# Dequantising weights by accumulating DMAs: negated zeros loaded first, the integer weights added on top

## The reference

```python
def dequantize(imatrix, scales, zeros, group_size, out_dtype):
    rs = jnp.repeat(scales, group_size, axis=0)
    rz = jnp.repeat(zeros, group_size, axis=0)
    return ((imatrix.astype(rs.dtype) - rz.astype(rs.dtype)) * rs).astype(out_dtype)
...
gate = jax.nn.silu(jnp.dot(x, gate_proj))
up = jnp.dot(x, up_proj)
return jnp.dot(gate * up, down_proj)
```

## Time and profile before

| | |
|---|---|
| three timed executions | 434.56, 435.77, 436.81 us, median 435.77 |
| profiled execution | 434.57 us |
| its span, first to last instruction | 432.8 us (1.8 us lie around it) |
| PE busy | 410.4 us, 95% of the span |
| DVE, ACT, POOL busy | 330.4, 330.5, 265.8 us |
| granted TensorE clock | 0.996 of full speed |

### The profile page before, as it was taken

One profiled execution on the slowest core, in us unless ns is written; L12 is line 12 of the kernel. 1 busy time (PEld: TensorE's weight loads), 2 busy tenths in 40 slices (PEclk: granted clock), 3 DMA queues, 4 the chain that ended last, 5 costly groups with the idle time before them and its releaser, 6 DMA issues.

```text
span 432.8 us, 10751 instructions
## 1 busy us (share of the span) xinstructions
PE 410.4 (95%) x4228; PEld 317.9 (73%) x4228; DVE 330.4 (76%) x582; ACT 330.5 (76%) x540; POOL 265.8 (61%) x264
## 2 busy tenths in 40 slices
PE   7878988999988999999999999999999999999994
PEld 5655666777856777777777878677877888888872
DVE  4778666998878778788887777787887667667676
ACT  2438898897877788687778888687888998988970
POOL 3335797899588654665473954755566555555561
PEclk9899999999999999999999999999999999999999
DMA  7677746966742000002010000000000000001003
GB/s 255 190 230 259 279 147 226 300 204 209 241 121 69 2 11 16 26 2 76 12 39 26 2 0 27 27 2 26 26 27 0 2 1 9 17 24 50 1 1 97
DMA packets 26792, 35.44 MB, mean 82 GB/s; under 512 B 1870, under 2 KB 18422, under 8 KB 26742
## 3 DMA queue, kind: packets, MB, share of 16 engines
q1 hardware_dynamic: 26434, 34.71, 24.5%
q10 hardware_dynamic: 244, 0.05, 0.1%
q0 software_dynamic: 64, 0.00, 0.0%
HBM read 30.56 MB, written 4.19 MB: 80 GB/s over the span
## 4 chain that ended last, share of the span: by engine, by line
PE 73%; DVE 9%; issue 6%; POOL 6%; ACT 4%; DMA 1%; POOLq 0%; SPq 0%; DVEq 0%; ACTq 0%
PE banks L764 20%; PE banks L766 19%; PE banks L777 10%; PE banks L778 9%; PE banks L663 4%; DVE yT L1039 2%; PE banks L703 2%; ACT banks L555 2%; PE banks L692 2%; PE banks L673 2%; PE banks L681 2%; POOL t_sb L416 1%; DVE st L925 1%; PE banks L722 1%; DVE qkT L943 1%
## 5 line engine op out<-in xcount | busy, mean ns | idle before, releaser
L555 ACT ACTIVATE banks<-banks,ratio 128x512 f32<-128x512 f32 x336 | 207.8, 664 | 34.9 <-PE banks L766 25.4
L1039 DVE SCALAR_TENSOR_TENSOR yT<-banks,sd,yT 128x512 f32<-128x512 f32 x208 | 154.1, 746 | 48.8 <-PE banks L778 48.1
L764 PE MATMUL banks<-xT,wgu 128*128 128x512 f32 x448 | 182.2, 407 | 5.2 <-DVE t_sb L1024 2.5
L766 PE MATMUL banks<-xT,wgu 128*128 128x512 f32 x448 | 175.1, 391 | 0.0
L416 POOL TENSOR_TENSOR t_sb<-t_sb,u_sb 128x512 f32<-128x512 f32 x56 | 72.7, 1298 | 63.1 <-DVE t_sb L1024 63.0
L764 PEld LDWEIGHTS banks<-xT,wgu 128*128 128x128 f32 x448 | 84.1, 188 | 27.6 <-issue 3.7
L766 PEld LDWEIGHTS banks<-xT,wgu 128*128 128x128 f32 x448 | 84.3, 188 | 15.2
L777 PE MATMUL banks<-hr,wd 128*128 128x512 f32 x224 | 89.3, 399 | 4.2 <-DVE yT L1039 2.3
L778 PE MATMUL banks<-hr,wd 128*128 128x512 f32 x224 | 87.5, 390 | 0.0
L429 POOL TENSOR_TENSOR hr<-t_sb,hr 128x512 fp32r<-128x512 f32 x56 | 73.1, 1305 | 5.1 <-ACT hr L577 0.7
L777 PEld LDWEIGHTS banks<-hr,wd 128*128 128x128 f32 x224 | 42.0, 188 | 19.3 <-DVE yT L1039 9.5
(11 more groups left out here) (93 smaller groups left out, 383.9 us busy)
## 6 DMA issues: line engine op xcount, KB each, us to landing
x_sb<-in_x SPq DMA_DIRECT2D x16, 256.0 KB, 5.2
out<-x_sb SPq DMA_DIRECT2D x16, 256.0 KB, 2.1
wgu_in<-in_L_ffn_gate_w SPq DMA_DIRECT2D x7, 512.0 KB, 5.7
z_in<-in_L_ffn_gate_z SPq DMA_DIRECT2D x7, 512.0 KB, 5.4
wgu_in<-in_L_ffn_up_w SPq DMA_DIRECT2D x7, 512.0 KB, 5.5
z_in<-in_L_ffn_up_z SPq DMA_DIRECT2D x7, 512.0 KB, 5.0
wd_in<-in_L_ffn_down_w SPq DMA_DIRECT2D x7, 512.0 KB, 5.3
z_in<-in_L_ffn_down_z SPq DMA_DIRECT2D x7, 512.0 KB, 4.6
```

The costliest lines, as they stand in the source:

```text
L555: act.activation(banks[:, bank, :], banks[:, bank, :], ACT.Copy, scale=ratio[:, m, g, it:it + 1]).then_inc(done[n % 2], 1)
L764: pe.matmul(banks[:, bank, :], w, xT[:, c % 2, 0, g, :], start=g == 0, stop=False, skip_group_check=True)
L766: pe.matmul(banks[:, bank, :], w, xT[:, c % 2, 1, g, :], start=False, stop=True, skip_group_check=True).then_inc(full[n % 2], 1)
L1039: dve.scalar_tensor_tensor(y, bank, sd[:, it, b:b + 1], y, ALU.mult, ALU.add).then_inc(s_free, 1)
```

## The change

The pass on the compute engines is gone. ACT's queue loads the three small tables of zeros (int32), ACT changes their sign and makes them f32, and SP writes them to a table `z_out` in HBM. From there SP loads each piece's zeros, broadcast to 128 partitions, straight into the place of the weights. Then POOL issues a DMA that reads the integer weights from HBM and adds them there (`accum_op=ALU.add`). PE waits for that DMA's semaphore. `z_in`, the two DVE waits on weights in `take_down` and all waits of SP for zero buffers are gone; the places in `piece_after` differ.

```diff
-    piece_after = {q: EARLY + i for i, q in enumerate((0, 2, 4, 9, 11, 14, 19, 21, 25, 27, 32, 33, 37, 38, 43, 44, 47))}
+    piece_after = {q: EARLY + i for i, q in enumerate((0, 2, 4, 8, 9, 12, 15, 16, 19, 21, 24, 26, 28, 31, 33, 36, 38))}
...
+            sync.wait_ge(s_zneg, 1)
+            sync.dma_start(z_out[:, :].rearrange("m (p n) -> p m n", n=64), z_neg).then_inc(s_zout, 16)
+            sync.wait_ge(s_zout, 16)
+
+            load_zeros(0)
+            load_zeros(1)
+            for k in range(2, EARLY + 1):
+                (load_ctx if k % 2 else load_x)(PRE + (k - 2) // 2)
+                sync.wait_ge(s_w[k - 2], 16)
                 load_zeros(k)
...
-                pool.tensor_tensor(piece_of(wgu_in, wd_in, k), piece_of(wgu_in, wd_in, k), piece_z(k),
-                                   ALU.subtract).then_inc(s_dif, 1)
+                pool.wait_ge(s_z[k], 16)
+                pool.dma_start(piece_of(wgu, wd, k), w.rearrange("(g p) n -> p g n", p=P),
+                               accum_op=ALU.add).then_inc(s_w[k], 16)
...
             norm1(0)
+            act.wait_ge(s_zraw, 48)
+            act.activation(z_neg, z_raw.bitcast(I32), ACT.Copy, scale=-1.0).then_inc(s_zneg, 1)
             norm1(1)
...
-            def convert(k):
-                act.wait_ge(s_dif, ready(k)[1])
-                act.copy(piece_of(wgu, wd, k), piece_of(wgu_in, wd_in, k)).then_inc(s_deqa, 1)
...
-                dve.tensor_tensor(piece_of(wgu, wd, k)[:, g, :], piece_of(wgu_in, wd_in, k)[:, g, :],
-                                  piece_z(k)[:, g, :], ALU.subtract).then_inc(s_deqv, 1)
```

## The result

The changed kernel takes 432.75 us (median of 7, 430.33 to 433.91) against 435.77 us before: ratio 0.9922, 95% interval 0.9894 to 0.9951. It is faster by 0.8%; the medians differ by 3.0 us. The profiled execution took 432.93 us, with a span of 431.1 us against 432.8, so this one shows 1.7 us of it.

The account below looks back on a forecast made before the run. PE was taken as the bound, idle in chunk 0 through dequantising; -1.3 (start) - 5.0 (chunk 0) + 1.0 (POOL) + 0.5 (prologue) = -4.8 us, giving 431.0 us as median, range 426.5 to 445.

Parts of the forecast that it names:

- near 97: Sign of being right: chunk 0, from `product` 0 to 14, takes near 97 us, against 101.33 before.
- the landing times grew: Sign of being wrong: landing times of the weight pieces that grow; no size given.
- Chunk 0, -5.0: Chunk 0: with dequantising gone from DVE and ACT, its whole loss against chunk 1's pace is recovered, -5.0 us.
- DMA time, "0": Weight pieces: accumulating DMAs of 3.1 us each stay hidden behind the matmuls, up to 4.2 us bearable; cost 0.
- PE would wait for `s_w`: Late places, if accumulating DMAs are too slow: at 4.6 us a piece 7 us late, about 438; chance 0.10.
- The start, -1.3: Step 0: without ACT's conversion the first `rescale` starts at about 46.2 instead of 47.54, -1.3 us.
- POOL's issue, 1.0: POOL's weight DMAs: each issue takes 1.0 us, 14 of them from place 6 to 38, leaving POOL 89% full.
- POOL's limit: Place 6 to 38: POOL becomes the bound at 1.4 us per issue.
- a fuller POOL (+1.0): Between `gated` and the down matmuls: POOL's fuller queue adds +1.0 us.
- Rival (1): Place 6 to 38: POOL becomes the bound; at 2.4 us per issue +7.6 us, 443; chance 0.17.
- The prologue, +0.5: Before place 0: `weigh(0)`, ending by 18.2, stays hidden; +0.5 us added for a new chain of five DMA landings.
- Rival (2): Place 6 to 38: DVE holds up POOL's issues, 1.9 us each; 436.4 us, no change; chance 0.06.

Follow-up runs that it names:

- no_zeros: Changed kernel with weight DMAs as plain converting copies, no zeros loaded and no POOL wait for them (result lacks the zeros): 425.4 us, ratio 0.9789.
- late_x: Changed kernel with the loads of x tiles 9 to 15 moved behind the last zeros in SP's program: 427.9 us, ratio 0.983.
- old_places: Changed kernel with the table of places of the kernel before: 434.0 us, ratio 0.9985.
- copy_only: Changed kernel with the weight DMAs as plain converting copies, without the addition; zeros loaded but not counted: 428.2 us, ratio 0.986.
- quiet_start: late_x with SP held before the zeros of piece 7 until PE has done `values(4)`: 427.9 us, ratio 0.984.
- late_x_split: late_x with each piece's accumulating DMA issued as two halves, 21 more issues for the same bytes: 434.7 us, ratio 0.9992.
- late_x_old_places: late_x with the table of places of the kernel before: 436.6 us, ratio 1.0026.

## Why the prediction was right, and where it was not

The direction and the interval held: 432.75 us in 426.5 to 445, faster. The forecast of 431.0 was 1.8 us too low; of the 4.8 us in the sum 3.0 came. The interval is wide: it reaches 9 us above the kernel before. And the parts agree less well than the sum. In the profile chunk 0 gave 0.7 us of 5.0 (100.6 us, where "near 97" was named as the sign of being right), the landing times grew, which was named as a sign of being wrong, and 0.6 us came from the prologue, where +0.5 was forecast. That the direction held with a stall of some 5 us in chunk 0 is in part luck.

**Chunk 0, -5.0.** The size was right as a ceiling, a little low: 6.3 us in no_zeros, 6.0 in late_x. The reading that led to it, chunk 0 against chunk 1 at the same points of the pattern, holds. In the changed kernel only 0.7 us of it arrived, and with the table of places of the kernel before (old_places) no gain in time is left: the new places are a part of what was gained.

**DMA time, "0".** This is the step that failed: it cost some 5 us (chunk 0 took 100.6 us, and 95.3 in late_x). The size of a piece was good: 3.1 us forecast for an accumulating one, 3.2 measured. The reduce rule of the Trainium skill (Collectives: The Full Stack, "The bandwidth ceiling"), half the rate of a copy, which was measured there on rings of four ranks, agrees with that against the 1.5 us of SP's copies; against a converting copy issued by POOL itself the addition costs 3.2 to 2.0, a factor of 1.6 here. What was wrong is the stretch over which I spread it. I divided by the 107 us from the first issue to the last use. But POOL issues its 17 pieces between 43.6 and 121 us: 17 x 3.2 = 54 us, zeros of 16 pieces at (0.173 x 431.1 - 0.089 x 425.8)/21 = 1.75 us (the SP queue with and without zeros) 28 us, 14 tiles some 11 us: 93 us of work for 77 us (an estimate; the shares of the two queues in that stretch, 0.657 and 0.464, give 87). So the engines were full and a queue grew. I also looked for the lateness only at PE's wait for the weights, where the lead is 11 places or more. The item with the short lead is the zeros: they share a queue with x tiles that nobody needs yet, and the wait for them stands on POOL, ahead of `rs` and `product`. "PE would wait for `s_w`" named the wrong waiter: PE waited for DVE's `yT`, DVE for POOL's `rs`, POOL for the zeros. PE does wait for the weights once the issues are late, as the two runs with the old table show.

**The start, -1.3.** The first `rescale` came as forecast, at 45.62, 0.1 us after its matmul (before, 1.4 us after). From place 0 to `product` 0, counted from PE's first matmul, only 11.2 - 10.9 = 0.3 us remained of it: PE's run of `score` had the gap of 1.01 us, whose cause is open. In copy_only, no_zeros and quiet_start, without the gap, that stretch took 9.6 us, 1.6 less than before: there the term is whole.

**POOL's issue, 1.0.** It took 1.31 us for gate and up and 1.2 for down, close below the 1.4 where I put POOL's limit. POOL was busy 50.5 us between `product` 0 and 8, forecast 50.9, and that agreement is luck: 13 pieces are issued in that stretch and not 14 (piece 20 stands behind `product` 8), each took 0.2 to 0.3 us more than forecast, and many overlapped the next instruction (the `product` of 75.19 starts 0.5 us before the issue of 74.36 is over). The cost of a fuller POOL (+1.0) can't be read off alone; late_x still got 6.0 of 6.3 us, so it is at most 0.3 where nothing stalls. Rival (1) did not come, but late_x_split shows that it was one doubling away. (At 2.0 us per issue its sum is 36.9 + 28.0 = 64.9, not 65.1.)

**The prologue, +0.5.** `weigh(0)` ran from 17.71 to 19.29, later than my 17.2 to 18.2, since the issue took 1.38 and overlapped it; PE's `mix(0)` came at 19.48. Hidden with 0.2 us to spare. Place 0 came 0.6 us earlier than before in this profile, within the spread of the prologues.

**Rival (2)**, DVE holding up POOL's issues: not seen. The issues took 1.29 to 1.38 us for gate and up and 1.18 to 1.26 for down, except where the next instruction of POOL overlapped them. The rule of the Trainium skill (SBUF — State Buffer, "Who interferes with whom") speaks of operations that this DVE program hardly has, so no run here tests it. The same section of the Trainium skill sets an operation with two SBUF inputs apart, which the prediction did not: by it such an operation contends with GpSimd's reads and was not seen to stall a DMA.

## What to carry to other kernels

When work moves to the DMA engines, add up their time over the stretch in which the transfers are issued, not over the one that ends with the last use, and count an accumulating one at its own price (3.2 us for 512 KB here, a converting copy 2.0). Then ask of each new wait what is queued behind it on the waiting engine, small operations for other engines included: here the lateness of a transfer went from POOL by a 128x1 operation to DVE and on to PE. Moving either the wait by up to four places or seven loads that are not needed yet out of the way brought some 4 us here. A table of places tuned for one mechanism is worth little for another: with the old table the gain could not be measured any more.

## What the runs showed of the hardware that was not expected

An accumulating DMA is dearer for its issuer too: POOL took 1.31 us for 128x4x256 with the addition, 0.81 us without. SP's issues are longer too in the crowded stretch: of zeros and tiles before, each took 0.3 to 1.0 us there, with the change up to 5.6; no run isolates the cause. And an idle of 3.3 us on PE was followed by some 5 us with a mean granted clock of 0.66, in part at 1.2 GHz, which added about 1.7 us to the loss; after the 5.4 us of idle in late_x_old_places the next 5 us had a mean of 0.50, the lower level throughout.
